# Some VectorE and GpSimd steps of a four-layer kernel put on the other engine or in another order, with one PSUM bank instead of two for the expert outputs

## The reference, cut to what matters

```python
xn = _layernorm(x, axis=-1)
s = _L2_attn_ref(xn, ...)
g = _silu(_L2_ffn_ref(xn, ...))
x = x + s * g
```

```python
q = l2norm(q) * qs
k = l2norm(k) * ksc
q, k = rotary_xpos(q, k)
...
a, g = jnp.split(h @ w1 + b1, 2, axis=-1)
h = a * jax.nn.gelu(g, approximate=False)
x = x + h @ w2 + b2
```

## Time and profile before

| what | value |
|---|---|
| median of 3 runs | 3853.13 us (3846.64 to 3855.7) |
| the profiled execution | 3853.13 us |
| its span, first to last instruction | 3851.2 us |
| PE busy | 3417.9 us, 89% |
| VectorE busy | 2534.8 us, 66% |
| ScalarE busy | 1773.9 us, 46% |
| GpSimd busy | 1023.6 us, 27% |
| granted TensorE clock, mean | 0.982 |

### The profile page before, as it was taken

One profiled execution on the slowest core, in us unless ns is written; L12 is line 12 of the kernel. 1 busy time (PEld: TensorE's weight loads), 2 busy tenths in 40 slices (PEclk: granted clock), 3 DMA queues, 4 the chain that ended last, 5 costly groups with the idle time before them and its releaser, 6 DMA issues. The chain is left out here.

```text
span 3851.2 us, 55779 instructions
## 1 busy us (share of the span) xinstructions
PE 3417.9 (89%) x20007; PEld 1781.9 (46%) x20007; DVE 2534.8 (66%) x5489; ACT 1773.9 (46%) x3776; POOL 1023.6 (27%) x895
## 2 busy tenths in 40 slices
PE   5998898888998899888988889988998889888877
PEld 2345544445344444455444453444444554445544
DVE  5666765676566765767666765667657676566675
ACT  1554544554444535545445544445354454455424
POOL 3033311332023410333113320234103331133324
PEclk8999999999999999999999999999999999999987
DMA  4100011102011020000111020110210001100130
GB/s 168 34 12 28 35 37 34 33 7 70 1 34 39 1 71 30 16 28 34 38 34 33 8 70 1 34 39 1 71 32 14 28 35 37 34 29 11 65 89 23
DMA packets 82300, 138.66 MB, mean 36 GB/s; under 512 B 10566, under 2 KB 56808, under 8 KB 79588
## 3 DMA queue, kind: packets, MB, share of 16 engines
q1 hardware_dynamic: 75972, 120.91, 9.7%
q10 hardware_dynamic: 3744, 6.61, 0.6%
q0 software_dynamic: 2304, 7.46, 0.6%
HBM read 105.06 MB, written 29.10 MB: 35 GB/s over the span
## 5 line engine op out<-in xcount | busy, mean ns | idle before, releaser
L650 DVE TENSOR_REDUCE nmax<-banks 128x1 f32<-128x512 f32 (+3 forms) x1216 | 759.2, 657 | 348.4 <-PE banks L460 211.4
L570 ACT ACTIVATE probs<-banks 128x512 f32<-128x512 f32 (+3 forms) x1024 | 475.9, 527 | 257.1 <-PE banks L479 181.1
L460 PE MATMUL banks<-ks,qs 72*128 72x512 bf16 (+3 forms) x1536 | 441.0, 332 | 75.2 <-DVE nmax L650 47.1
L479 PE MATMUL banks<-qs,ks 74*128 74x512 bf16 (+3 forms) x1536 | 445.2, 330 | 36.8 <-ACT probs L570 14.0
L113 PE MATMUL banks<-filler,identb 128*128 128x512 bf16 x1824 | 456.6, 379 | 9.3 <-PEq L443 9.3
L460 PEld LDWEIGHTS banks<-ks,qs 72*128 72x128 bf16 x1536 | 141.9, 98 | 356.2 <-DVE nmax L650 198.4
L570 ACT ACTIVATE early<-banks 128x256 f32<-128x256 f32 (+3 forms) x512 | 196.1, 440 | 167.1 <-PE banks L479 166.5
L113 PEld LDWEIGHTS banks<-filler,identb 128*128 128x128 bf16 x1824 | 173.5, 98 | 208.1 <-issue 54.6
L1510 ACT ACTIVATE probs<-banks,nm 128x192 f32<-128x192 f32 x512 | 172.1, 421 | 206.6 <-DVE nm L1462 206.6
L1544 POOL TENSOR_TENSOR probs<-probs,inv 128x768 f32<-128x768 f32 x128 | 187.0, 1466 | 253.5 <-DVE inv L1472 253.5
L479 PEld LDWEIGHTS banks<-qs,ks 74*128 74x128 bf16 x1536 | 141.7, 98 | 226.2 <-ACT probs L570 75.5
(11 more groups left out here) (523 smaller groups left out, 6739.4 us busy)
## 6 DMA issues: line engine op xcount, KB each, us to landing
qs<-parts_scratch SPq DMA_DIRECT2D x300, 96.0 KB
ks<-parts_scratch SPq DMA_DIRECT2D x288, 96.0 KB
parts_scratch<-parts SPq DMA_DIRECT2D x50, 384.0 KB, 2.5
shared<-in_w_h SPq DMA_DIRECT2D x17, 1024.0 KB, 7.5
shared<-in_w SPq DMA_DIRECT2D x26, 256.0 KB, 3.8
qs<-max_parts SPq DMA_DIRECT2D x192, 4.0 KB
xn<-in_x SPq DMA_DIRECT2D x9, 256.0 KB, 2.8
factor_scratch<-g SPq DMA_DIRECT2D x8, 256.0 KB, 2.3
```

The source lines that it names most:

```text
L460: mm = nc.tensor.matmul(K.ps[:, b, i * keys:(i + 1) * keys], K.qs[0:72, 4 * g + j, t * P:(t + 1) * P], K.ks[0:72, 4 * g + j, 0:keys], star ...
L479: mm = nc.tensor.matmul(K.ps[:, b, q0:T], K.ks[0:KR, h, k * P:(k + 1) * P], K.qs[0:KR, h, q0:T], start=True, stop=not on_tensor)
L570: nc.scalar.activation(probs[:, 4 * (q % QUADS) + m % 4, q0:T], K.ps[:, bank("second", m), q0:T], ACT.Exp, scale=scale).then_inc(exped, 1)
L650: nc.vector.tensor_reduce(nmax[:, t, h:h + len(heads)], K.ps[:, n % 2, 0:len(heads) * keys].rearrange("p (j k) -> p j k", k=keys), AX.X, A ...
```

## The change

- `local_qkv`: the queries of tiles 0 to 2 are scaled by VectorE, each in the turn of the next tile, ahead of its rotation; GpSimd keeps the query scale of the last tile only. The clip is a `tensor_scalar` instead of a `scalar_tensor_tensor`.
- `Glu`, both uses: GpSimd no longer adds the bias; VectorE adds it after the product.
- `GluThenQkv`: for tiles 2 and 3 VectorE scales the queries too, behind the keys.
- `LastGlu`: `TURN_FILLERS` goes from 6 to 0.
- `experts`: `down(e)` always writes bank 7 and so waits until expert e-1 was added; the router compares and weighs with eight `tensor_scalar` of 8 elements instead of two operations of 64; `magnitudes` comes right behind the router; ACT takes the exponential one half earlier; the end of the softplus goes from one VectorE operation to two GpSimd operations behind the convolution.

```diff
@@ local_qkv, vector
-            x = ssq[:, t, :, :]
-            ch.do(nc.vector.scalar_tensor_tensor(x, x, 1e-24, x, ALU.max, ALU.max))
+            ch.do(nc.vector.tensor_scalar(ssq[:, t, :, :], ssq[:, t, :, :], 1e-24, None, ALU.max))
             nc.vector.reciprocal(ssq[:, t, :, :], ssq[:, t, :, :]).then_inc(clipped, 1)
+            if t:
+                dve.wait_ge(rn_ready, t)
+                dve.wait_ge(added, 2 * t - 1)
+                scale_heads(nc.vector, t - 1, 0).then_inc(q_scaled, 1)
@@ local_qkv, gpsimd
-                pool.wait_ge(rn_ready, t + 1)
-                pool.wait_ge(added, 2 * t + m + 1)
-                scale_heads(nc.gpsimd, t, m).then_inc((q_scaled, k_scaled)[m], 1)
+            pool.wait_ge(rn_ready, t + 1)
+            if t < NT - 1:
+                pool.wait_ge(added, 2 * t + 2)
+                scale_heads(nc.gpsimd, t, 1).then_inc(k_scaled, 1)
+            else:
+                pool.wait_ge(added, 2 * t + 1)
+                pool.wait_ge(q_scaled, NT - 1)
+                scale_heads(nc.gpsimd, t, 0).then_inc(q_scaled, 1)
@@ Glu
         dve.wait_ge(self.down, 1)
-        dve.wait_ge(self.y_biased, 1)
+        ch.do(nc.vector.tensor_tensor(K.y[:, :, :], K.y[:, :, :],
+                                      K.ps[:, self.down_bank, :].rearrange("p (t d) -> p t d", t=NT), ALU.add))
         nc.vector.tensor_tensor(K.y[:, :, :], K.y[:, :, :],
-                                K.ps[:, self.down_bank, :].rearrange("p (t d) -> p t d", t=NT),
+                                K.b2_down[L][:, :].unsqueeze(1).to_broadcast([P, NT, D]),
                                 ALU.add).then_inc(self.y_ready, 1)
...
-        yield self.TURN_STEP
-        pool.wait_ge(self.yturned, 1)
-        nc.gpsimd.tensor_tensor(K.y[:, :, :], K.y[:, :, :],
-                                K.b2_down[self.L][:, :].unsqueeze(1).to_broadcast([P, NT, D]),
-                                ALU.add).then_inc(self.y_biased, 1)
@@ GluThenQkv, vector
                 if t >= self.LATE:
                     dve.wait_ge(self.late_added, t - self.LATE + 1)
                     scale(1).then_inc(self.late_scaled, 1)
-                else:
-                    dve.wait_ge(self.added, t + 1)
-                    scale(0).then_inc(self.q_scaled, 1)
+                dve.wait_ge(self.added, t + 1)
+                scale(0).then_inc(self.q_scaled, 1)
@@ LastGlu
-    TURN_FILLERS = 6
+    TURN_FILLERS = 0
@@ experts, tensor: down(e)
-                    if e == 1:
-                        pe.wait_ge(top_read, 1)
-                    elif e >= 2:
-                        pe.wait_ge(used, e - 1)
+                    if e:
+                        pe.wait_ge(used, e)
...
-                            mm = nc.tensor.matmul(K.ps[:, 7 - e % 2, t * P:(t + 1) * P],
-                                                  h[:, e % 2, c, t * P:(t + 1) * P],
+                            mm = nc.tensor.matmul(K.ps[:, 7, t * P:(t + 1) * P], h[:, e % 2, c, t * P:(t + 1) * P],
@@ experts, scalar
-                    if n == 2 * NOW - 2:
+                    if n == 3:
@@ experts, vector: router, then the magnitudes at e == 0 instead of e == 1
-                    ch.do(nc.vector.tensor_tensor(eq[:, :, :, :], number, chosen, ALU.is_equal))
-                    ch.do(nc.vector.tensor_tensor(eq[:, :, :, :], eq[:, :, :, :],
-                                                  pr[:, :, :].unsqueeze(3).to_broadcast(every), ALU.mult))
+                    for r in range(2):
+                        for t in range(NT):
+                            ch.tick(nc.vector.tensor_scalar(eq[:, r, t, :], K.iota8[:, :], idf[:, t, r:r + 1],
+                                                            pr[:, r, t:t + 1], ALU.is_equal, ALU.mult))
+                    ch.wait()
...
-                softplus()
@@ experts, gpsimd, behind the convolution
+                pool.wait_ge(sig_done, 1)
+                pool.wait_ge(abs_ready, 1)
+                nc.gpsimd.tensor_scalar(zt[th, :], zt[th, :], 0.0, None, ALU.max).then_inc(floored, 1)
+                pool.wait_ge(floored, 1)
+                pool.wait_ge(ln_done, 1)
+                nc.gpsimd.tensor_tensor(aet[th, :], zt[th, :], za[th, :], ALU.add).then_inc(aet_ready, 1)
```

More of the change, by code:

```diff
@@ L1563, in __init__ @@
          self.gelu_done, self.hid_ready, self.down, self.yturned, self.shifted) = K.pool[24:37]
-        self.y_ready, self.y_biased = K.pool[37], K.pool[18]
+        self.y_ready = K.pool[37]
         self.y_bank, self.back_bank, self.turn_bank, self.down_bank = (7, 0, 1, 6) if alone else (7, 6, 7, 6)
         self.up_banks = [(2, 3), (4, 5)] if alone else [(6, 7)]
-        self.filler_bank = 3
         self.rows = [P, P, HID2 - 2 * P]
@@ L2273, in add_out, with memory_part @@
                     ch.wait()
[L2275 to L2285 removed]
+                def memory_part(e):
+                    if e == 0:
+                        dve.wait_ge(projected, 1)
+                        ch.do(nc.vector.tensor_scalar(zt[th, :], K.ps[64:96, 5, :], K.b3_aet[th, 0:1], None, ALU.add))
+                        nc.vector.scalar_tensor_tensor(za[th, :], zt[th, :], -1.0, zt[th, :], ALU.mult,
+                                                       ALU.max).then_inc(abs_ready, 1)
                 for e in range(NOW):
@@ L2301, in _ @@
                         add_out(e - 1)
-                    if e == 1:
-                        magnitudes()
-                softplus()
+                    memory_part(e)
                 add_out(NOW - 1)
```

38 lines of the change are left out of this document (12 added, 26 removed).

## The result

| | before | changed |
|---|---|---|
| median of four runs each, us | 3852.91 (3846.64 to 3855.7) | 3949.22 (3941.83 to 3949.91) |
| ratio, 95% interval | 1 | 1.0248 (1.023 to 1.0266) |
| profiled execution, span, us | 3851.2 | 3937.7 |
| mean granted clock | 0.982 | 0.973 |

The kernel is 96 us slower. The forecast was 3895 us with a range up to 3918, so the direction was right and the size was not.

The account below looks back on a forecast made before the run. Bound taken: a chain passing from engine to engine with little slack. Edits 5.4 us per batch, times 8 = 43, plus 6 for the fillers' gap, minus 7 for existing half-clock stretches: +42 on 3853.13, 3895 us; range 3870 to 3918.

Parts of the forecast that it names:

- local_qkv: In local_qkv, VectorE's query scale meets GpSimd's key scale, delaying the rotation 0.45 us in three tiles: +1.35 per batch.
- bias additions: In both Glu uses, VectorE's added operation behind the down product lengthens the chain: +0.70 us each per batch.
- late query scale: In GluThenQkv's last tile, the query scale on VectorE ends earlier than on GpSimd: -0.15 us per batch.
- experts: Router, magnitudes and the last down product's wait lengthen the path to the loop's end: +2.8 us per batch, bounds +1.1, +3.9.
- LastGlu's gap and all other clock terms: Lower clock behind LastGlu's gap without fillers, +6 us in all; existing half-clock stretches reduced, 7 us off.
- the two tail rows: At local_qkv's tail, VectorE's scale ends 0.54 us after GpSimd's; taken as the model for the new query scale.
- "free" and "blocked": Router in experts unhindered or held by GpSimd, ending 2.4 us later; experts +1.8 or +3.6 us per batch.
- the row that I weighed against blocking: In experts, the router's two operations fit into 0.97 us with GpSimd at work throughout; evidence for an unblocked router.
- I take 6 us in all: Clock cost of LastGlu's gap without fillers: about 2 us in three of eight batches.
- I take 7 off: Half-clock stretches already in most batches, more than chance would give, expected to become fewer: -7 us, bounds -21, +5.
- the clock falls in every batch without the fillers: Rival, 13%: LastGlu's gap lowers the clock in all batches, +22 us instead of +6, nothing taken off: 3918 us.
- the strict reading I weighed: At LastGlu's gap, two short PE idle spells with transposes between cost nothing, making that clock term 0.

Follow-up runs that it names:

- router_only: Kernel before with the router's two operations written as eight tensor_scalar of 8 elements; clean experts stage 25.15 us (22.2 to 22.4 before).
- experts_undone: Changed kernel with the old experts put back; 3907.9 us, ratio 1.0139.
- scales_only: Kernel before with local_qkv's changed clip and query scale and the first feed-forward's late query scale on VectorE; 3875.0 us, ratio 1.0049.
- experts_only: Kernel before with the changed experts and nothing else; 3889.3 us, ratio 1.0099.
- warm_after: Changed kernel with LastGlu's six fillers back and more before second-score products in two attentions, third expert's up products and last down product; 3899.9 us, ratio 1.0119.
- warm_before: Kernel before with added TensorE fillers before single second-score products in two attentions, none elsewhere; 3845.3 us, ratio 0.9977.
- router_back: Changed kernel with the router's two operations over all tiles in place of the eight; 3927.4 us, ratio 1.019.
- best: Kernel before with warm_before's fillers, five more around the causal attentions' output projection, the tensor_scalar clip and the late query scale on VectorE; 3837.0 us, ratio 0.9957.
- delay_before: Kernel before with five more TensorE fillers at the end of last_feed_forward; 3857.9 us, ratio 1.0017.
- fillers_back: Changed kernel with LastGlu's six fillers put back and nothing else; 3935.3 us, ratio 1.0217.
- delay_after: Changed kernel with five more TensorE fillers at the end of last_feed_forward; 3953.5 us, ratio 1.0267.

## Why the prediction was wrong

| term, 8 batches, us | forecast | measured in spans |
|---|---|---|
| local_qkv | +10.8 | +8.4 |
| bias additions | +11.2 | +11.4 |
| late query scale | -1.2 | -2.6 |
| experts | +22.4 | +30.8 |
| VectorE late at the jump back | none | +4 |
| LastGlu's gap and all other clock terms | -1 | +34.5 (rest) |
| sum | +42 | +86.5 |

**The chains were right.** The first bias arrives 0.72 later, the second 0.71. In local_qkv the new scale ends 0.55 behind GpSimd's (0.54 forecast) and the last scale ends 1.34 later (1.35); 0.3 of it is absorbed before the first maximum of local attention, so +1.05 arrives. The rotation's start moved by what the two tail rows show.

**experts was mis-sized at one choice and one bound.** I put the router between "free" and "blocked" and took the middle. The rows stood for blocked: an operation of 44 elements had been. The seventh of the eight starts at 1887.02 and ends at 1888.38, with GpSimd's addition (1887.09 for 1.27). Over all batches the shortest, the median and the longest, in ns:

```profile
L2252 DVE TENSOR_SCALAR eq<-iota_s,idf,pr x64: 276/342/1361, 500.4 to 3734.5; 128x8 f32<-128x8 f32 x64
```

The other seven take 0.28 to 0.65 each, although GpSimd works beside them too. The first six start beside its multiplication (L2304, a tensor_scalar, 1885.43 for 1.57), and that holds them for a part of its time only: the first ends 0.71 behind its start (0.65 long), the second and third take 0.28 and end inside it, the fourth and fifth end 0.03 and 0.04 behind its end (0.59 and 0.41 long). In all eight batches only the seventh, beside the addition (a tensor_tensor), stands for GpSimd's whole operation. The router of the kernel before ran beside the same multiplication:

```profile
1847.30 1.57 POOL L2313 TENSOR_SCALAR tap<-raw,conv_w_s 96x512 f32<-96x512 f32 x1
...
1847.36 0.69 DVE L2255 TENSOR_TENSOR eq<-iota_s,idf 128x64 f32<-128x64 f32 x1
1848.09 0.23 DVE L2256 TENSOR_TENSOR eq<-eq,pr 128x64 f32<-128x64 f32 x1
```

So the row that I weighed against blocking, two operations in 0.97 us with GpSimd at work throughout, spoke of GpSimd's tensor_scalar and not of its addition. Each of the two readings fits its own neighbour. The Trainium skill, "SBUF — State Buffer", section "Who interferes with whom", has it as a lock held for a whole instruction; the trace agrees beside GpSimd's additions and scales (tensor_tensor), for 8 and for 16 elements, and not for the whole of its tensor_scalar, beside which these shorter ones ended; there the measurement decides. The path I followed for what came behind was PE's; `router_only` shows that it is VectorE's, without room. The blocked path gave +3.6, the clean stage has +3.85; I had put 2.8 into the sum.

**The clock terms failed, and they are most of the miss (35.5 of 44.5 us in spans; experts is 8.4).** The step reads "I take 6 us in all" for the fillers' gap and "I take 7 off" for the existing stretches. Both treat a stretch at 0.50 as an independent event worth 2.7 us at most once a batch. The runs show something else. A batch of 454.4 clean us (447.9 and the terms above, an estimate) became one of 460.7 to 461.0, in five of seven; one of 450.1 became 457.3 (`experts_undone`), one of 448.6 became 454.0 (`scales_only`), one of 451.7 became 454.0 (`experts_only`). My reading, which no run isolates: when the length of a batch changes, all its spells with little work shift together against whatever decides on the clock, and the pattern that results repeats in batch after batch, since the batches have become equally long. The rival "the clock falls in every batch without the fillers" had the right idea for one place (1.6 us x 7 = 11, where it took 22) and missed the two others: the first feed-forward, which no edit touches there and which alone costs 3.1 x 7 = 22 us, and the new idle spell in experts, 1.8 x 5 = 9. My reason for taking 7 off, that most batches had a stretch already and so there was more to lose than to gain, was wrong: the kernel before had 37.5 us at 0.50 in seven batches, and there was room for 101.6.

The 34.5 of the table is a remainder. The changed kernel has 64 us more at 0.50 in seven batches; where 3.4 us at that level cost 1.6 and 6.8 cost 3.1, these make some 30, an estimate. That the clock is the cause is shown by two pairs: the changed kernel with and without more fillers (3949.2 and 3899.9), and `scales_only` with and without them (3875.0 and 3845.6). And where fillers hold the level in both kernels, the change costs 55 us (`warm_after` against `warm_before`), near the 52 that the table's terms without the clock add up to. The Trainium skill, "TensorE: Matmul & The Clock Gate", section "Part 1: The HAM clock gate (the 'warmup' mystery)", ties the low level to idleness; the strict reading I weighed, by which short idle spells between products cost nothing, does not fit the window 1752.80:1756.80 above, in which PE was busy 2.82 of 4.00 us, with waits like the 0.68 and 0.83 shown, before the level fell. The same section says that the hardware's watch runs by itself and does not begin with the kernel, which fits a pattern that depends on where a batch stands in time; no run here shows that directly.

**What stays open.** Why batches settle just at 450.6, 454.0, 457.3 and 460.8, and which of them a given edit leads to: the delays of 1.07 and 0.51 us could not tell it, and `router_back` keeps 460.9 with 1.7 us less work. Three of the four timed runs of the changed kernel were some 10 us longer than the one profiled; what those 10 us are was not seen. And the clock term as a whole stays without a rule: the runs show what the falls cost and that fillers take most of them away (17.5 us at 0.50 are left in seven batches of `warm_after`, against 101.6), not how to forecast where they come.

## What to carry to other kernels

Before an edit is priced, list the places where TensorE's level falls or nearly falls, and treat the clock as one property of the whole loop: an edit that lengthened an iteration by 0.73 us cost 3 per iteration (`scales_only`). Filling TensorE's waits in just those spells was cheap here, made this kernel 0.2% faster (0.4% with five fillers more and the late query scale, `best`), and makes later edits measurable for what they are. And where VectorE and GpSimd held each other up, look which operation the other engine has there: beside GpSimd's additions and scales (tensor_tensor, 512 elements), count a VectorE operation with two inputs in SBUF or in tensor_scalar's form as held until they end, as the rows here have it; beside its tensor_scalar of 1.57 us they show holds of a part of it only. Splitting one such operation into eight gives the other engine seven more chances to come between.

## What the runs showed of the hardware that I had not expected

- The distance from batch to batch took few values where it was steady: 450.6 (`delay_before`), 454.0 (`experts_only`, `scales_only`, `router_only`), 457.3 (`experts_undone`) and 460.7 to 461.0 (the changed kernel, `fillers_back`, `router_back`).
- Savings can vanish: 1.7 us less in experts left the batch at 460.9 (`router_back`).
- After the jump back to the loop's head VectorE started 2.3 to 2.8 us behind PE in every batch of the changed kernel, and also in `fillers_back` (2.3 to 2.8), `delay_after` (2.4 to 2.7) and `warm_after` (2.5 to 3.3), but 0.42 in `experts_only`, `experts_undone` and `router_back`. The sequencer's row shows VectorE standing between its branch (1905.41) and its next instruction (1908.01). It cost 0.4 to 0.9 us per batch. Each of the two halves of the change alone is free of it. One thing goes with it in the traces: in the first 3.5 us behind PE's first product the instruction queue q14 moved four packets in each batch of the changed kernel and of `fillers_back`, and three in the kernel before, `experts_only`, `experts_undone` and `router_back`. That VectorE waited for instructions would fit; it is not shown, and the cause is open.
- A tensor_scalar of 8 elements took up to 1.36 us beside a GpSimd addition, and one of 16 elements 1.19; beside GpSimd's tensor_scalar of 96x512 (1.57 us) it took 0.28 to 0.65.
